# A graph attention layer: chunks attended to three slots later, turned tokens alternating with v, and another order on VectorE

## The chip, the cores and the metric

The kernel runs on one NeuronCore of one Trainium2 chip. The metric is the device time of one execution in microseconds (us). A core has TensorE (PE in the rows; PEld is its weight loads), VectorE (DVE), ScalarE (ACT), GpSimd (POOL) and SyncE (SP), which here only issues DMAs (SPq). Each engine works through its own instructions in the order written and waits on semaphores.

## What is computed

128 graphs of 128 nodes with 384 features go through a layer norm with relu, and one attention layer with 12 heads of 32 features, masked by the adjacency; the input is added at the end. Cut to what matters:

```python
h = relu(layernorm(x))                        # 128 graphs x 128 nodes x 384
q, k, v = (split_heads(h @ W + b) for W, b in ((Wq, bq), (Wk, bk), (Wv, bv)))
scores = einsum('bhqd,bhkd->bhqk', q, k) / sqrt(32) + beta * adj
scores = where(adj > 0, scores, -9e15)
out = x + merge_heads(softmax(scores) @ v)
```

## The kernel before, in words

**Words used.** A *group* is four graphs, 512 tokens; there are 32. A *chunk* is one graph and four of its heads, so a group has 12 chunks. A *step* s projects group s and attends to group s - 1; there are 33, of which the first only projects and the last only attends. Most steps are the body of a loop over pairs of steps (`run_steps`). A step has 12 *slots*, and in each slot TensorE does four things in this order: the scores of chunk n (L436, four matmuls), the turning (transposition) of the exponentials of chunk n - 1 (`turn_probs`, L444, four), a piece of the projections (`PIECES[u]`, L424), and the values of chunk n - 2 (`values_of`, L459 to L461, twelve short matmuls).

**Projections.** `UNITS` lists 13 units of a step: q and k, three each, nine matmuls of 512 columns per unit; v, four, nine matmuls of 384 columns; and three "turn" units, the transposed tokens of the next group (L404), four transposes each. The units are cut into twelve pieces of about equal cost. A unit is gathered in one of three banks (`ps_p`), so that `bank_free` lets unit o begin only when the unit three before it has been read out: for q and k that is VectorE's low part, for v ScalarE's copy, for a turn VectorE's low part of the tokens.

**Two parts.** q, k, the tokens and the probabilities are each kept as a high part, written by ScalarE, and a low part, the rest, written by VectorE (`low_part` L604, `turn_low` L594, `p_low` L630). v is copied by ScalarE (L525) and split by GpSimd (`split_v`, L318 and L320).

**A chunk's way.** TensorE's scores; VectorE adds the mask and takes the row maxima, head by head (`bias_scores`, L624); ScalarE takes the exponentials (`exps`, L510); TensorE turns them into `ps_t`, of which there is one bank; ScalarE takes the high part (`p_high`, L535) and VectorE the low one (`p_low`). `turn_probs` of a chunk waits for the exponentials of that chunk and for the `p_low` of the chunk before:

```python
pe.wait_ge(exp_done, HPC * (n + 1))
wait(pe, p_low_done, n)
```

After a graph's third chunk VectorE inverts the sums (L640) and scales (L645), GpSimd adds x (`add_x`, L326) and SyncE stores (L248).

**The spread.** The scores need q and k stacked by head. SyncE copies them there from SBUF to SBUF (`spread`, L241), 12 DMAs for q and 12 for k in a step, each set once the low parts of all three units are done. The scores of the first chunk of a group wait for both:

```python
if u == 0:
    pe.wait_ge(q_in, 16 * 3 * HPC * s)
    pe.wait_ge(k_in, 16 * 3 * HPC * s)
```

In the order before, that is slot 0 of the step after the one that projected the group. `q_st` and `k_st` have two buffers, by the parity of the step. On SyncE's queue a step is: the last store of two groups back, the load of x, the spread of q, a store, the load of the adjacency, the spread of k, two stores.

**VectorE in a slot.** Before: `bias_scores`, the inversion if a graph has ended, `p_low`, the scaling, one half of the mask (slots 4 and 7), `moments` (L571) of the next group's tokens, the low part of the unit that ended in the slot before, `variance` (L577).

Of the kernel before, what the change touches and what calls it, by code (L numbers as in the profile page):

```python
# [21 lines left out]
def graph_attention_kernel(nc, x, adj, wq, bq, wk, bk, wv, bv, beta, out):  # L22
# [3 lines left out]
    HPC = P // HD  # L26
# [4 lines left out]
    SLOTS = G * CH  # L31
    SCALE = float(HD) ** -0.5
# [8 lines left out]
             + [("v", 0), ("v", 1), ("turn", 0), ("v", 2), ("turn", 1), ("turn", 2), ("v", 3)])  # L41
# [37 lines left out]
    with ExitStack() as ctx:  # L79
# [132 lines left out]

        def rows_of(row):

            return row.rearrange("(o d) -> o d", o=1).broadcast_to([P, D])
# [6 lines left out]
        def _(sp):  # L222
# [27 lines left out]
            def step(s, par, looped=False):  # L250
                proj, attend = has(s, looped, 0, STEPS - 1), has(s, looped, 1, STEPS)
                if has(s, looped, 2, STEPS):
                    store(s - 2, G - 1)
# [15 lines left out]
                if attend:  # L269
                    store(s - 1, 1)  # L270
                    store(s - 1, 2)
                if s is STEPS:
                    store(s - 1, 3)
# [6 lines left out]
        def _(pool):  # L280
# [47 lines left out]
            def step(s, par, looped=False):  # L328
                proj, attend = has(s, looped, 0, STEPS - 1), has(s, looped, 1, STEPS)
                if proj:  # L330
                    add_bias(s, par, 0)
                    add_bias(s, par, 1)
                if has(s, looped, 2, STEPS):
                    add_x(s - 2, par, G - 1)
                if proj:
                    add_bias(s, par, 2)
                    add_bias(s, par, 3)
                if has(s, looped, 0, STEPS - 2):
                    rstd_of(s + 1)
                    normalise(s + 1, 1 - par)  # L340
                if attend:
                    add_x(s - 1, 1 - par, 0)
                if proj:
                    split_v(s, par, 0)
                if attend:
                    add_x(s - 1, 1 - par, 1)
                if proj:
                    split_v(s, par, 1)
                    split_v(s, par, 2)
                if attend:  # L350
                    add_x(s - 1, 1 - par, 2)
                if proj:
                    split_v(s, par, 3)
                if s is STEPS:
# [22 lines left out]
        def _(pe):  # L377
# [50 lines left out]
            def scores(s, par, u):  # L428

                j, c, n = u // CH, u % CH, SLOTS * (s - 1) + u  # L430
                if u == 0:
                    pe.wait_ge(q_in, 16 * 3 * HPC * s)
                    pe.wait_ge(k_in, 16 * 3 * HPC * s)
                wait(pe, biased_done, HPC * (n - 1))
                for i in range(HPC):
                    mm = pe.matmul(ps_s[u % 2][:, i * N:(i + 1) * N], q_st[0:STACK, 1 - par, i, c, j * N:(j + 1) * N],  # L436
                                   k_st[0:STACK, 1 - par, i, c, j * N:(j + 1) * N], start=True, stop=True)
# [9 lines left out]
            def values_of(g, vp, v, n, odd):  # L447
# [6 lines left out]
                for i in range(HPC):  # L454
# [3 lines left out]
                    first, second = v1[:, vp, j, h, :], v2[:, vp, j, h, :]  # L458
# [5 lines left out]
            def step(s, par, looped=False):  # L464
                proj, attend = has(s, looped, 0, STEPS - 1), has(s, looped, 1, STEPS)
                ahead = has(s, looped, 0, STEPS - 2)
                drain = 2 if not looped and s == STEPS else 0
                for u in range(SLOTS + drain):
                    n = SLOTS * (s - 1) + u
                    if attend and u < SLOTS:  # L470
                        scores(s, par, u)
                    if attend and u - 1 < SLOTS and (looped or n >= 1):
                        turn_probs(n - 1, (u - 1) % 2)
# [7 lines left out]
                    if attend and (looped or n >= 2):  # L481
                        late = u < 2
                        values_of(s - 1 - late, par if late else 1 - par, (u - 2) % SLOTS, n - 2, u % 2)
# [17 lines left out]
        def _(act):  # L501
            act.dma_start(xs[:, 0], x_v[0]).then_inc(x_in[0], 16)

            def exps(s, u):

                n, odd = SLOTS * (s - 1) + u, u % 2
# [252 lines left out]
```

## Time and profile before

| | us |
|---|---|
| median of 3 runs (lowest, highest) | 1191.81 (1189.29, 1191.97) |
| the profiled execution, its time | 1193.08 |
| its span in the trace | 1191.3 |
| TensorE busy in the span | 1068.0 (90%) |
| VectorE busy | 957.0 (80%) |
| ScalarE busy | 894.7 (75%) |
| GpSimd busy | 570.9 (48%) |
| mean granted TensorE clock | 0.969 |

The span is from the first to the last record of the trace; the run's own time is 1.8 us more. "Busy" counts the time between an instruction's start and end, so a matmul that overlaps the next counts with its drain; the start-to-start distance of matmuls (their pitch) tells what TensorE can do. A clock of 1.00 is 2.4 GHz, and half of that 1.2 GHz.

### The profile page before, as it was taken

How to read it: one execution, taken by the hardware profiler on the slowest of the kernel's cores; microseconds unless marked ns; L12 is line 12 of the kernel's file. 1: busy time of each engine (PE TensorE's matmuls, PEld its weight loads, DVE VectorE, ACT ScalarE, POOL GpSimd, SP SyncE). 2: the span in 40 equal slices, each digit the busy share in tenths (PEclk: the TensorE clock that was granted, in tenths of full speed). 3: DMA queues.
4: the chain of work that ended last, by engine and by line, in shares of the span. 5: the costliest groups of instructions: out<-in, count | busy, mean ns of one | idle time of the engine just before them, and what ended most of it. 6: DMA issues, size and time to landing. Idle time of an engine off the chain costs nothing.

```text
span 1191.3 us, 38643 instructions
## 1 busy us (share of the span) xinstructions
PE 1068.0 (90%) x10959; PEld 904.1 (76%) x10959; DVE 957.0 (80%) x4343; ACT 894.7 (75%) x2343; POOL 570.9 (48%) x756
## 2 busy tenths in 40 slices
PE   2799889999999999999999999999999999999875
PEld 1677777877787887778788777778877787888764
DVE  5478778888888888888888888878888888888764
ACT  2377768877787887777788787778877777887764
POOL 3735535445544545454454455454545445454421
PEclk9899999999999999999999999999999999999985
DMA  4434345444444544434554444454444345443330
GB/s 141 112 94 114 110 110 141 122 116 118 115 107 134 142 123 116 119 109 109 136 141 118 114 113 115 115 137 129 118 118 115 105 127 143 129 117 93 80 96 28
DMA packets 91030, 138.14 MB, mean 116 GB/s; under 512 B 15600, under 2 KB 66288, under 8 KB 90864
## 3 DMA queue, kind: packets, MB, share of 16 engines
q1 hardware_dynamic: 90336, 135.85, 42.4%
q14 instruction: 149, 1.22, 0.3%
q10 hardware_dynamic: 528, 0.79, 0.2%
q8 instruction: 17, 0.28, 0.1%
HBM read 35.91 MB, written 25.17 MB: 51 GB/s over the span
## 4 chain that ended last, share of the span: by engine, by line
PE 57%; SPq 14%; DVE 12%; issue 11%; DMA 5%; ACT 1%; POOL 1%; DVEq 1%; POOLq 0%; ACTq 0%
PE ps_p L424 35%; SPq L241 13%; PE ps_t L444 9%; PE ps_s L436 6%; DMA k_st<-kT 4%; DVE biased L624 4%; DVE kT L604 3%; PE ps_o L459 2%; PE ps_o L460 2%; PE ps_o L461 2%; DVE on L645 1%; DVE hT L594 1%; DMA beta_col<-in_L_gnn_beta 1%; PE ps_p L404 1%; ACT probs L510 1%
## 5 line engine op out<-in xcount | busy, mean ns | idle before, releaser
L624 DVE CUSTOM_DVE_ANT_0 biased<-ps_s,mask 128x128 f32<-128x128 f32 x1536 | 351.7, 284 | 181.0 <-PE ps_s L436 166.0
L510 ACT ACTIVATE probs<-biased,neg_max 128x128 f32<-128x128 f32 x1536 | 487.0, 391 | 7.4 <-DVE neg_max L624 7.0
L424 PE MATMUL ps_p<-hT,w 128*128 128x512 f32 x1728 | 475.2, 415 | 3.7 <-DVE w L733 3.7
L535 ACT ACTIVATE pT<-ps_t 128x512 f16<-128x512 f32 x384 | 229.3, 597 | 244.0 <-PE ps_t L444 242.9
L424 PEld LDWEIGHTS ps_p<-hT,w 128*128 128x128 f32 x1728 | 314.1, 193 | 61.5 <-issue 3.9
L630 DVE TENSOR_TENSOR pT<-ps_t,pT 128x512 f16<-128x512 f32 x384 | 256.9, 669 | 17.7 <-ACT pT L535 17.5
L444 PE MATMUL ps_t<-ident,probs 128*128 128x128 f32 x1536 | 241.6, 281 | 16.0 <-ACT probs L510 15.7
L326 POOL TENSOR_TENSOR on<-on,xb 128x384 f32<-128x384 f32 x128 | 128.5, 1004 | 264.4 <-DVE on L645 262.1
L424 PE MATMUL ps_p<-w,hT 128*128 128x384 f32 x1152 | 243.9, 348 | 0.0
L436 PE MATMUL ps_s<-k_st,q_st 96*128 96x128 f16 x1536 | 150.9, 221 | 55.6 <-DMA k_st<-kT 49.4
L424 PEld LDWEIGHTS ps_p<-w,hT 128*128 128x128 f32 x1152 | 193.5, 189 | 2.7
L318 POOL CAST v<-v_f 128x384 f16<-128x384 f32 x128 | 64.7, 505 | 267.4 <-ACT v_f L525 250.0
L459 PEld LDWEIGHTS ps_o<-v,pT 128*128 128x128 f16 x1536 | 123.8, 97 | 81.5 <-issue 53.9
L444 PEld LDWEIGHTS ps_t<-ident,probs 128*128 128x128 f32 x1536 | 166.2, 144 | 21.0 <-ACT probs L510 20.8
L459 PE MATMUL ps_o<-v,pT 128*128 128x33 f16 x1536 | 160.9, 181 | 1.1 <-DVE pT L630 1.1
L460 PE MATMUL ps_o<-v,pT 128*128 128x33 f16 x1536 | 155.7, 178 | 0.0
L461 PE MATMUL ps_o<-v,pT 128*128 128x32 f16 x1536 | 155.7, 177 | 0.0
L436 PEld LDWEIGHTS ps_s<-k_st,q_st 96*128 96x128 f16 x1536 | 90.6, 97 | 59.7 <-issue 59.7
L460 PEld LDWEIGHTS ps_o<-v,pT 128*128 128x128 f16 x1536 | 126.1, 97 | 1.1
L311 POOL TENSOR_TENSOR xb<-xs,bv_row 128x384 f32<-128x384 f32 x128 | 126.5, 1011 | 0.0
L624 DVE DVE_READ_ACCUMULATOR2_ANT neg_max<- 128x1 f32 x1536 | 126.5, 82 | 0.0
L461 PEld LDWEIGHTS ps_o<-v,pT 128*128 128x128 f16 x1536 | 124.2, 96 | 0.0
(59 smaller groups left out, 1073.0 us busy)
## 6 DMA issues: line engine op xcount, KB each, us to landing
q_st<-qT SPq DMA_DIRECT2D x384, 96.0 KB, 2.2
k_st<-kT SPq DMA_DIRECT2D x384, 96.0 KB, 2.1
out<-on SPq DMA_DIRECT2D x128, 192.0 KB, 1.9
xs<-in_x SPq DMA_DIRECT2D x31, 768.0 KB, 4.6
adjs<-in_adj SPq DMA_DIRECT2D x32, 256.0 KB, 2.9
xs<-in_x ACTq DMA_DIRECT2D x1, 768.0 KB, 6.9
k_st<-in_L_gnn_Wq SPq DMA_DIRECT2D x1, 576.0 KB, 5.3
k_st<-in_L_gnn_Wk SPq DMA_DIRECT2D x1, 576.0 KB, 7.4
```

The lines of the kernel that those rows point to most:

```text
L241: sp.dma_start(dst[HD * b:HD * (b + 1), par, i], src[HD * i:HD * (i + 1), part]).then_inc(landed, 16)
L326: pool.tensor_tensor(on[:, j % 2, :], on[:, j % 2, :], xb[:, par, j, :], ALU.add).then_inc(added, 1)
L424: mm = pe.matmul(dst, stationary, moving, start=m == 0, stop=m == MMS - 1)
L436: mm = pe.matmul(ps_s[u % 2][:, i * N:(i + 1) * N], q_st[0:STACK, 1 - par, i, c, j * N:(j + 1) * N], k_st[0:STACK, 1 - par, i, c, j * N:(j ...
L444: mm = pe.transpose(ps_t[:, i * N:(i + 1) * N], probs[:, odd, i, :], ident[:])
L459: pe.matmul(o, high, first, start=True, stop=False)
L460: pe.matmul(o, low, first, start=False, stop=False)
L461: mm = pe.matmul(o[:, 0:HD], high, second, start=False, stop=True)
L510: act.activation(probs[:, odd, i, :], biased[:, odd, i, :], ACT.Exp, bias=neg_max[:, odd, i:i + 1], scale=-1.0).then_inc(exp_done, 1)
L535: act.activation(pT[:, odd, 0], ps_t[:].rearrange("p (h q) -> p h q", q=N), ACT.Copy).then_inc(p_high_done, 1)
L624: dve.tensor_tensor_reduce(out=biased[:, odd, i, :], in0=ps_s[odd][:, i * N:(i + 1) * N], in1=mask[:, 1 - par, u // CH, :], scale=-1.0, sc ...
L630: dve.tensor_tensor(pT[:, odd, 1], ps_t[:].rearrange("p (h q) -> p h q", q=N), pT[:, odd, 0], ALU.subtract).then_inc(p_low_done, 1)
```

## The change

Scores of a chunk now come three slots later (`LAG = CH`): a group's chunks are scored in slots 3 to 11 of the step after its projection and in slots 0 to 2 of the one after that, and turning, values and scaling follow as before, one, two and three slots behind. The units `turn` and v alternate. On VectorE the low parts of projected units stand between `bias_scores` and `p_low`. The stores on SyncE and the additions and v splits on GpSimd are put where their data now come. The number of operations is the same. The core of the diff (`values_of`, `exps`, and `bias_scores` take their chunk from `chunk` likewise):

```diff
+    LAG = CH
...
     UNITS = ([("q", c) for c in range(CH)] + [("k", c) for c in range(CH)]
-             + [("v", 0), ("v", 1), ("turn", 0), ("v", 2), ("turn", 1), ("turn", 2), ("v", 3)])
+             + [("v", 0), ("turn", 0), ("v", 1), ("turn", 1), ("v", 2), ("turn", 2), ("v", 3)])
...
+        def chunk(s, par, u, behind, looped):
+
+            v = u - LAG - behind
+            back = 2 if v < 0 else 1
+            n = SLOTS * (s - 1) + v
+            if v >= SLOTS or (not looped and not 0 <= n < CHUNKS):
+                return None
+            return n, s - back, par if back == 2 else 1 - par, v % SLOTS
...
                 if has(s, looped, 2, STEPS):
-                    store(s - 2, G - 1)
+                    store(s - 2, 1)
+                    store(s - 2, 2)
+                if proj:
+                    spread(s, par, "q")
+                if has(s, looped, 2, STEPS):
+                    store(s - 2, 3)
                 if has(s, looped, 0, STEPS - 3):
...
-                if proj:
-                    spread(s, par, "q")
-                if attend:
-                    store(s - 1, 0)
                 if has(s, looped, 0, STEPS - 2):
                     sp.wait_ge(mask_done, s + 1)
                     sp.nop(nofuse=True)
                     sp.dma_start(adjs[:], adj_v[s + 1]).then_inc(adj_in, 16)
+                if attend:
+                    store(s - 1, 0)
                 if proj:
                     spread(s, par, "k")
...
+                for u in range(SLOTS + (LAG + 2 if s is STEPS else 0)):
+                    scored, turning, valued = (chunk(s, par, u, behind, looped) for behind in range(3))
+                    if scored:
+                        scores(*scored, (u - LAG) % 2)
+                    if turning:
+                        turn_probs(turning[0], (u - LAG - 1) % 2)
...
+                    scored, turning, _, valued = (chunk(s, par, u, behind, looped) for behind in range(4))
+                    ended = valued is not None and valued[3] % CH == CH - 1
+                    if scored:
+                        bias_scores(*scored, (u - LAG) % 2)
+                    if proj and u >= 1:
+                        low_parts(s, par, u - 1, ahead)
                     if ended:
-                        invert_sums(s - 1 - late, j)
-                    if attend and (looped or n >= 1) and u - 1 < SLOTS:
-                        p_low(n - 1, (u - 1) % 2)
+                        invert_sums(valued[1], valued[3] // CH)
+                    if turning:
+                        p_low(turning[0], (u - LAG - 1) % 2)
                     if ended:
-                        scale_out(s - 1 - late, j)
+                        scale_out(valued[1], valued[3] // CH)
...
                     if ahead and u < G:
                         moments(s + 1, 1 - par, u)
-                    if proj and u >= 1:
-                        low_parts(s, par, u - 1, ahead)
                     if ahead and u < G:
                         variance(s + 1, u)
```

In the rows of the order below (those that only handle registers are left out), `L624 ISA biased` is the masked score of one head and `L624 ISA neg_max` the read of its maximum; the lines of the changed kernel are some ten higher (L633 for L624, L639 for L630, L614 for L604, L604 for L594, L440 for L424, L452 for L436, L460 for L444, L420 for L404). VectorE in slot 2 of a step, from the last head's masked scores on, before:

```order
L624 ISA biased,neg_max<-ps_s,mask 128x128
L624 ISA neg_max 128x1
L640 RECIPROCAL inv_sum<-ps_o 128x12 [waits scaled,pv_done]
L630 TENSOR_TENSOR pT<-ps_t,pT 128x512 [waits p_high_done]
L645 TENSOR_TENSOR on<-ps_o,inv_sum 128x384 [waits stored1,inverted]
L571 BN_STATS stats<-xs 128x6 [waits var_done,x_in0]
L604 SCALAR_TENSOR_TENSOR qT<-ps_p,bias_qk,qT 128x512 [waits qk_high]
L575 REGISTER_ALU [waits rstd_done]
L577 BN_AGGR mean_var<-stats 128x2 [waits stats_done]
L196 REGISTER_ALU [waits scores_done]
L624 ISA biased,neg_max<-ps_s,mask 128x128 [waits exp_done]
```

and now:

```order
L633 ISA biased,neg_max<-ps_s,mask 128x128
L633 ISA neg_max 128x1
L614 SCALAR_TENSOR_TENSOR qT<-ps_p,bias_qk,qT 128x512 [waits qk_high]
L649 RECIPROCAL inv_sum<-ps_o 128x12 [waits scaled,pv_done]
L639 TENSOR_TENSOR pT<-ps_t,pT 128x512 [waits p_high_done]
L199 ISA [waits inverted]
L654 TENSOR_TENSOR on<-ps_o,inv_sum 128x384 [waits stored0]
L581 BN_STATS stats<-xs 128x6 [waits var_done,x_in0]
L585 REGISTER_ALU [waits rstd_done]
L587 BN_AGGR mean_var<-stats 128x2 [waits stats_done]
L199 REGISTER_ALU [waits scores_done]
L633 ISA biased,neg_max<-ps_s,mask 128x128 [waits exp_done,mask_done]
```

The low part of q (`qT`) stood after the scaling and the moments, between BN_STATS and BN_AGGR; it now stands ahead of `pT`, which is `p_low`, and BN_AGGR directly follows BN_STATS.

TensorE in slot 10 before, between the turned probabilities and the values:

```order
L444 MATMUL ps_t<-ident,probs 128x128 [waits p_low_done,exp_done]
L444 MATMUL ps_t<-ident,probs 128x128 x3
L424 MATMUL ps_p<-w,hT 128x384 x5
L404 MATMUL ps_p<-ident,hn 128x128 [waits normed,v_copied]
L404 MATMUL ps_p<-ident,hn 128x128 x3
L404 MATMUL ps_p<-ident,hn 128x128 [waits normed,h_low]
L404 MATMUL ps_p<-ident,hn 128x128 x3
L459 MATMUL ps_o<-v,pT 128x33 [waits p_low_done]
```

and now slots 8 and 10 in the same stretch:

```order
L460 MATMUL ps_t<-ident,probs 128x128 [waits p_low_done,exp_done]
L460 MATMUL ps_t<-ident,probs 128x128 x3
L440 MATMUL ps_p<-w,hT 128x384 x4
L418 ISA [waits qk_low]
L420 MATMUL ps_p<-ident,hn 128x128 [waits normed]
L420 MATMUL ps_p<-ident,hn 128x128 x3
L440 MATMUL ps_p<-w,hT 128x384 [waits qk_low]
L440 MATMUL ps_p<-w,hT 128x384 x2
```

```order
L460 MATMUL ps_t<-ident,probs 128x128 [waits p_low_done,exp_done]
L460 MATMUL ps_t<-ident,probs 128x128 x3
L440 MATMUL ps_p<-w,hT 128x384 x8
L420 MATMUL ps_p<-ident,hn 128x128 [waits normed,v_copied]
L420 MATMUL ps_p<-ident,hn 128x128 x3
```

The two turns that stood next to each other are apart, and v1 begins in slot 8 behind the first turn, where it waits for the bank of k's third unit (`qk_low`).

SyncE's queue in the loop, from the spread of q to the spread of k, before:

```order
L241 DMA q_st<-qT 32x1536 x11
L248 ISA [waits added]
L248 DMA out<-on 128x384
L266 ISA [waits mask_done]
L266 DMA adjs<-in_adj 128x4x128
L196 REGISTER_ALU [waits scores_done]
L241 DMA k_st<-kT 32x1536 [waits qk_low]
```

and now:

```order
L253 DMA q_st<-qT 32x1536 x11
L260 ISA [waits added]
L260 DMA out<-on 128x384
L275 ISA [waits xb_done,normed]
L275 DMA xs<-in_x 128x4x384
L279 ISA [waits mask_done]
L279 DMA adjs<-in_adj 128x4x128
L260 ISA [waits added]
L260 DMA out<-on 128x384
L199 REGISTER_ALU [waits scores_done]
L253 DMA k_st<-kT 32x1536 [waits qk_low]
```

The load of x and of the adjacency and the store of the group's first graph stand between the two spreads.

## Rows read from the trace of the kernel before

**Rows 1.** The page: the span.

```profile
span 1191.3 us, 38643 instructions
```

**Rows 2.** Busy time by stretch: us, PE, PEld, DVE, ACT, POOL, PEclk, DMA share, GB/s.

```profile
413.90:448.60 34.70, 32.36 (x342) 27.54 (x342) 29.40 (x135) 27.64 (x73) 17.75 (x24) 1.00 0.46 122
518.00:552.70 34.70, 33.75 (x342) 28.59 (x342) 27.97 (x134) 27.29 (x73) 16.01 (x21) 0.95 0.43 114
```

**Rows 3.** Waits of the whole span: us in total, times, longest us.

```profile
PEld ps_s L436 <- issue: 59.7, 34, 6.1
PE ps_s L436 <- DMA k_st<-kT: 49.4, 29, 5.8
```

**Rows 4.** Timeline of PE, slot 10 to slot 2: start, us, instructions, idle before.

```profile
409.19 0.66 PE L404 MATMUL ps_p<-ident,hn 128*128 128x128 f32 x4 [0.70 <-DVE hT L594]
...
409.99 0.38 PE L436 MATMUL ps_s<-k_st,q_st 96*128 96x128 f16 x4
...
413.99 0.39 PE L436 MATMUL ps_s<-k_st,q_st 96*128 96x128 f16 x4 [1.30 <-DMA k_st<-kT]
...
416.62 0.38 PE L436 MATMUL ps_s<-k_st,q_st 96*128 96x128 f16 x4
...
416.84 0.61 PE L444 MATMUL ps_t<-ident,probs 128*128 128x128 f32 x4
...
419.24 0.38 PE L436 MATMUL ps_s<-k_st,q_st 96*128 96x128 f16 x4
```

**Rows 5.** The chain of waits around 414 to 440: start, us until the next piece.

```profile
414.84 1.63 PE ps_p L424 x7
...
436.17 1.74 PE ps_p L424 x10
...
439.42 0.44 PE ps_p L404 x4
```

**Rows 6.** Timeline of SP's queue: the spreads of k, first and last of 30.

```profile
87.10 7.51 SPq L241 DMA_DIRECT2D k_st<-kT  x12
...
404.64 7.51 SPq L241 DMA_DIRECT2D k_st<-kT  x12
...
1102.32 8.39 SPq L241 DMA_DIRECT2D k_st<-kT  x12
```

**Rows 7.** The page: DMA issues, the spread of k, median us to landing.

```profile
k_st<-kT SPq DMA_DIRECT2D x384, 96.0 KB, 2.1
```

**Rows 8.** Timeline of DVE, slots 0 and 2.

```profile
416.19 0.55 DVE L571 BATCH_NORM_STATS2 stats<-xs 128x6 f32<-128x384 f32 x1
416.85 0.18 DVE L577 BATCH_NORM_AGGREGATE mean_var<-stats 128x2 f32<-128x6 f32 x1
...
419.86 0.29 DVE L624 CUSTOM_DVE_ANT_0 biased<-ps_s,mask 128x128 f32<-128x128 f32 x1 [0.31 <-PE ps_s L436]
...
420.86 0.63 DVE L630 TENSOR_TENSOR pT<-ps_t,pT 128x512 f16<-128x512 f32 x1
421.40 0.55 DVE L645 TENSOR_TENSOR on<-ps_o,inv_sum 128x384 f32<-128x384 f32 x1
421.86 0.55 DVE L571 BATCH_NORM_STATS2 stats<-xs 128x6 f32<-128x384 f32 x1
422.33 0.73 DVE L604 SCALAR_TENSOR_TENSOR qT<-ps_p,bias_qk,qT 128x512 f16<-128x512 f32 x1
422.98 0.17 DVE L577 BATCH_NORM_AGGREGATE mean_var<-stats 128x2 f32<-128x6 f32 x1
423.07 0.26 DVE L624 CUSTOM_DVE_ANT_0 biased<-ps_s,mask 128x128 f32<-128x128 f32 x1
```

**Rows 9.** Timeline of ACT in slot 1.

```profile
417.49 0.60 ACT L535 ACTIVATE pT<-ps_t 128x512 f16<-128x512 f32 x1 [0.77 <-PE ps_t L444]
```

**Rows 10.** Timeline of PE at the first and the last attention of a step.

```profile
60.95 0.58 PE L436 MATMUL ps_s<-k_st,q_st 96*128 96x128 f16 x4 [5.82 <-DMA k_st<-kT]
...
1148.63 0.38 PE L436 MATMUL ps_s<-k_st,q_st 96*128 96x128 f16 x4 [2.39 <-issue]
```

**Rows 11.** Timeline of ACT in the last step.

```profile
1152.46 0.60 ACT L535 ACTIVATE pT<-ps_t 128x512 f16<-128x512 f32 x1 [1.21 <-PE ps_t L444]
1152.96 1.26 ACT L510 ACTIVATE probs<-biased,neg_max 128x128 f32<-128x128 f32 x4
1155.43 0.60 ACT L535 ACTIVATE pT<-ps_t 128x512 f16<-128x512 f32 x1 [1.21 <-PE ps_t L444]
```

More of the change, by code:

```diff
@@ L329, in step @@
                 proj, attend = has(s, looped, 0, STEPS - 1), has(s, looped, 1, STEPS)
+                older = has(s, looped, 2, STEPS)
+                if has(s, looped, 1, STEPS):
+                    split_v(s - 1, 1 - par, G - 1)
                 if proj:
@@ L344, in step @@
                     split_v(s, par, 0)
+                    split_v(s, par, 1)
                 if attend:
@@ L426, in project, with scores @@
                     mm.then_inc(proj_done, 1)
[L428 to L433, printed above, removed]
+            def scores(n, g, gp, v, odd):
+                j, c = v // CH, v % CH
+                if v == 0:
+                    pe.wait_ge(q_in, 16 * 3 * HPC * (g + 1))
+                    pe.wait_ge(k_in, 16 * 3 * HPC * (g + 1))
                 wait(pe, biased_done, HPC * (n - 1))
                 for i in range(HPC):
-                    mm = pe.matmul(ps_s[u % 2][:, i * N:(i + 1) * N], q_st[0:STACK, 1 - par, i, c, j * N:(j + 1) * N],
-                                   k_st[0:STACK, 1 - par, i, c, j * N:(j + 1) * N], start=True, stop=True)
+                    mm = pe.matmul(ps_s[odd][:, i * N:(i + 1) * N], q_st[0:STACK, gp, i, c, j * N:(j + 1) * N],
+                                   k_st[0:STACK, gp, i, c, j * N:(j + 1) * N], start=True, stop=True)
                 mm.then_inc(scores_done, 1)
@@ L457, in values_of @@
                     high, low = pT[:, odd, 0, i, :], pT[:, odd, 1, i, :]
-                    first, second = v1[:, vp, j, h, :], v2[:, vp, j, h, :]
+                    first, second = v1[:, gp, j, h, :], v2[:, gp, j, h, :]
                     pe.matmul(o, high, first, start=True, stop=False)
@@ L464, in step @@
             def step(s, par, looped=False):
[L465 to L473, printed above, removed]
+                proj, ahead = has(s, looped, 0, STEPS - 1), has(s, looped, 0, STEPS - 2)
+                for u in range(SLOTS + (LAG + 2 if s is STEPS else 0)):
[4 more added lines that the diff above has]
+                        turn_probs(turning[0], (u - LAG - 1) % 2)
                     if proj:
@@ L480, in step @@
                                 turn(s + 1, ps_p[BANK[par][o]], UNITS[o][1])
-                    if attend and (looped or n >= 2):
-                        late = u < 2
-                        values_of(s - 1 - late, par if late else 1 - par, (u - 2) % SLOTS, n - 2, u % 2)
+                    if valued:
+                        values_of(*valued, (u - LAG) % 2)
             pe.wait_ge(consts_set, 3)
@@ L538, in step @@
             def step(s, par, looped=False):
-                proj, attend = has(s, looped, 0, STEPS - 1), has(s, looped, 1, STEPS)
-                ahead = has(s, looped, 0, STEPS - 2)
-                drain = 1 if not looped and s == STEPS else 0
-                for u in range(SLOTS + drain):
-                    n = SLOTS * (s - 1) + u
-                    if attend and (looped or n >= 1):
-                        p_high(n - 1, (u - 1) % 2)
-                    if attend and u < SLOTS:
-                        exps(s, u)
+                proj, ahead = has(s, looped, 0, STEPS - 1), has(s, looped, 0, STEPS - 2)
+                for u in range(SLOTS + (LAG + 1 if s is STEPS else 0)):
+                    scored, turning = (chunk(s, par, u, behind, looped) for behind in range(2))
+                    if turning:
+                        p_high(turning[0], (u - LAG - 1) % 2)
+                    if scored:
+                        exps(scored[0], (u - LAG) % 2)
                     if proj:
```

48 lines of the change are left out of this document (20 added, 28 removed).

## The prediction, made before the changed kernel ran

> **What bounds the kernel now.** I read the page, then the busy time by stretch, the waits, and the timeline of one step engine by engine. The span is 1191.3 us [rows 1]. In a step in the middle TensorE is busy for 32.36 of 34.70 us, VectorE for 29.40 and ScalarE for 27.64, at clock 1.00 [rows 2]: TensorE is nearest to the end and VectorE is not far. What TensorE waits for shows in the waits: the scores that open a step wait for the spread of k (49.4 us over 29 times, and under "issue" 59.7 us over 34 times for the same matmuls' weight loads; these overlap) [rows 3].
>
> What can a step cost at least? From the pitch of TensorE's instructions: seven matmuls of 512 columns go by in 1.63 us, 0.233 each; ten of 384 in 1.74, 0.174 each; four transposes in 0.44 [rows 5]. Scores take 0.22 us up to the turning [rows 4]. A slot with seven 512s is 2.62 us long (416.62 to 419.24) [rows 4], so scores, turning and values together are 2.62 - 1.63 = 0.99. A step is 54 x 0.233 + 36 x 0.174 + 3 x 0.44 + 12 x 0.99 = **32.0 us** of TensorE's work. From the spread of k in step 1 to that in step 30, 29 steps, it took 1102.32 - 87.10 = 1015.2 us [rows 6], **35.0 us** each. So 3.0 us of a step are waits. Two are seen: about 0.7 at the third turn, which waits for the first turn's low part to free its bank, and 1.3 (in other steps more) at the first scores of the next step, slot 11 having begun at 409.99 and lasting 2.56 by the pitch, with the next at 413.99, 1.4 late [rows 4]. Some steps run a stretch at half clock as well: mean clock 0.95 in one, against 1.00 [rows 2]. That clock loss follows waits and should go with them.
>
> **The change part by part.** *Three slots later.* The spread of k leaves SyncE from 404.64 for 7.51 us; its twelfth DMA is issued some 0.6 before that ends, at 411.5, and lands 2.1 later, at 413.6, and the scores begin at 413.99 [rows 4, 6, 7]. Now the scores need it three slots, 8 us, later. But the spread is itself set later: behind the store of the first graph, whose scaling is in VectorE's slot 8, with an addition on GpSimd of 1 us. I put its start at about 27 us into the step, its landing at 27 + 7.5 - 0.6 + 2.1 = 36, and its use at 34 + 8 = 42. Some 5 to 6 us are left, so this wait goes: -1.4 us or more a step.
>
> *Turns apart.* The second turn needs the bank of v0, long copied; the third that of v1. The 0.7 goes. Yet in slot 8 v1 now needs k's third unit, whose low part VectorE takes only in slot 8. Scores begin; 0.62 later VectorE can begin (419.24 to 419.86) [rows 4, 8]; masked scores 0.85, low part 0.65 [rows 8]; so the bank is free at 2.2, while TensorE is there after 0.22 + 0.36 + 4 x 0.174 + 0.44 = 1.7. A wait of 0.5, and as VectorE comes 0.25 late into slot 8 (below) and TensorE restarts slowly, **0.9**. In slot 9 v2 needs the first turn's low part in the same way: **0.2**.
>
> *Low parts first.* In slot 2 VectorE's masked scores and inversion take 1.00 us (419.86 to 420.86), `p_low` and scaling 1.00, moments 0.47, low part 0.65, variance 0.09 [rows 8]: 3.21, the next masked scores starting at 423.07. Now BN_AGGR follows BN_STATS at once, and such a pair takes 0.66 (416.19 to 416.85) plus 0.09 [rows 8] instead of 0.56: 0.2 more in slots 2 and 3. So slot 2 is 3.4 and slot 3 2.9, against TensorE's 2.85 and 2.62: VectorE enters slot 3 0.55 and slot 4 0.8 late. Before, that delay hit low parts, which nobody waited for soon. Now `p_low` ends in slot 3 at 0.62 + 0.55 + 0.85 + 0.65 + 0.69 = 3.4 after the scores, and TensorE wants to turn the next chunk at 2.62 + 0.22 = 2.84: a wait of **0.6** in slot 4. In slot 5 the same sum leaves **0.3**, and in slots 8 and 0, which follow slots with the mask or with an ended graph, **0.2** each. Where VectorE is on time, the sum is 0.62 + 0.85 + 0.65 + 0.69 = 2.81, just in time: this edit has no margin.
>
> *ScalarE.* It takes the turned chunk 0.65 after the turning starts (416.84 to 417.49) [rows 4, 9], then the exponentials; 0.65 + 0.5 + 1.3 = 2.45 is below a slot, so it hides behind TensorE. GpSimd is busy for 17.75 of 34.70 [rows 2]; its additions and splits in the new places have several us before their use. The load of x is behind the spread of q and a store, and still some 12 us early. All three cost nothing; should GpSimd be late, the store and then the spread of k are late next, with the 5 us above.
>
> **The step.** 32.0 + 0.6 + 0.3 + 0.9 + 0.2 + 0.2 = 34.2 (the wait in slot 0 of 0.2 is partly the same delay; I count it once with slot 8's), so **34.2** against 35.0.
>
> **The ends.** At the first attention TensorE has idled for 5.82 us [rows 10]; three slots of projections, 22 x 0.233 = 5.1 us, now fit there. Counted from 60.95, step 1 ends three slots, 8.1 us, sooner. The last step has 15 chunks instead of 12 to pass through the chain ScalarE and TensorE alone, 2.97 us each (1152.46 to 1155.43) [rows 11]: 8.9 more. Step 31 has no turns, -1.5 as before.
>
> **Sum.** Before, 60.95 to 1148.63 [rows 10] is 31 steps at 35.1. Now 60.95 + 31 x 34.2 - 8.1 - 1.5 + (1191.3 - 1148.63) + 8.9 = 1163. The profiled run's time was 1.8 above its span and 1.3 above the median of the runs, so the median should be **1164**, 28 us or 2.3% less.
>
> **Bounds.** The unknown is what TensorE waits in a step under the new order. If VectorE's delay is half of what I work out, the step is 33.1 and the time 1164 - 31 x 1.1 = 1130. If each of the waits is a quarter longer and the restarts cost more, it is 34.85: 1184.
>
> **Rivals.** *TensorE runs free.* If VectorE catches up (its 29.4 us of work fit into 32), the step is about 32.4 and the time 1164 - 31 x 1.8 = 1108. Against it: VectorE's work is not even, and slots 2 to 5 hold 11.4 us of it against 10.7 of TensorE's. 0.13.
>
> *A page's rule.* The row of the mid step gives the weight loads 27.54 us against the matmuls' 32.36 [rows 2]. The Trainium skill (Perfetto Trace Analysis, Identifying the Most-Contended Engine) holds matmul busy time to be a poor measure of TensorE's distance from its limit and weight-load busy time to be a good one. By it TensorE has 7 us to give, VectorE's 29.4 would bound the step, and the time would be 1164 - 31 x 4.8 = 1015. The pitch speaks against that here: 0.233 us a matmul with nothing waited for [rows 5]. 0.01.
>
> *Slower: the turning always waits for `p_low`.* The low part ahead of it stands in nine slots. Each costs at most its own 0.65: 5.9 us, a step of 37.9 and 1164 + 31 x 3.7 = 1279. It turns slower once these nine waits exceed 0.35 us each (35.1 - 32.0 = 3.1). The place is L444 waiting for L630. For it: the sum above is 2.81 against 2.84. Against it: only slots 2 to 5 are fuller than TensorE's. 0.07.
>
> *The wait stays.* If the spread of k starts over 5 us later than I put it (its store or the addition ahead is late), the change does not do what it says: a step stays at 35.0, about 1190, the last step's 8.9 made up by the first's 8.1. 0.05.
>
> **The numbers.** My forecast has 0.74. A difference of 0.3% (3.6 us) is about what runs of this kernel can tell. Faster: 0.71 of the forecast's 0.74, with 0.14 of the first two rivals, is 0.85, and mild forms of the two slow rivals make it 0.87. Same: 0.05. Slower: 0.08. 1130 to 1184 leaves out the free case, the slow one and the tails.
>
> **What would show it.** Right: no wait of the first scores for DMA k_st in the loop; spreads of k 34.2 us apart; TensorE waiting for DVE pT (`p_low`) at the turning in slots 4 and 5, and for DVE kT at v1; the clock 1.00 in every step; the last step 8.9 us longer. Wrong: waits for k_st remain; steps of 32.4, with hardly a wait of TensorE; or waits of the turning in all slots.

## The result and the profile after

| | before | changed kernel |
|---|---|---|
| median, us (lowest, highest) | 1191.89 (1189.29, 1193.88) | 1257.4 (1255.43, 1263.74) |
| ratio, 95% interval | 1 | 1.0562 (1.0529 to 1.0595) |
| span in the trace | 1191.3 | 1254.4 |
| TensorE, VectorE, ScalarE busy | 90%, 80%, 75% | 88%, 78%, 71% |
| mean granted TensorE clock | 0.969 | 0.961 |

The change made the kernel 5.6% slower; 1164 was forecast, with 1130 to 1184 as the range. The page of the changed kernel:

```profile
span 1254.4 us, 38643 instructions
...
PE 1103.8 (88%) x10959; PEld 920.9 (73%) x10959; DVE 972.7 (78%) x4343; ACT 896.2 (71%) x2343; POOL 581.5 (46%) x756
...
q14 instruction: 97, 0.79, 0.2%
```

Every engine has as many instructions as before, and all are idle for longer. TensorE's busy time is 36 us more than the 1068.0 before, for the same matmuls. Its waits (us in total, times, longest):

```profile
PEld ps_t L460 <- ACT probs L522: 102.6, 58, 4.5
PE ps_t L460 <- ACT probs L522: 71.3, 28, 4.3
DVE biased L633 <- issue: 69.2, 41, 5.2
ACT probs L522 <- DVE neg_max L633: 66.8, 41, 4.5
PE ps_t L460 <- DVE pT L639: 34.4, 72, 0.8
PE ps_p L440 <- DVE kT L614: 9.8, 31, 0.7
```

The wait of the scores for k's spread (49.4 us [rows 3]) is gone, as forecast, and the small waits for `p_low` and for k's low part are there. But one chain has grown: TensorE's turning waits 71.3 us for ScalarE's exponentials (15.7 before), these wait for VectorE's row maxima, and VectorE waits for nothing the profile knows ("issue"). SyncE's queue shows where it falls (start, duration of the spreads of k):

```profile
376.11 7.52 SPq L253 DMA_DIRECT2D k_st<-kT  x12
417.54 7.50 SPq L253 DMA_DIRECT2D k_st<-kT  x12
452.11 7.53 SPq L253 DMA_DIRECT2D k_st<-kT  x12
493.52 7.50 SPq L253 DMA_DIRECT2D k_st<-kT  x12
```

The steps are no longer alike: 34.6 us and 40.6 to 41.4 us in turn. The busy time of one of each (columns as in [rows 2]):

```profile
417.54:452.11 34.57, 33.15 (x344) 27.79 (x343) 29.83 (x136) 27.66 (x75) 17.80 (x24) 1.00 0.46 122
452.11:493.52 41.41, 35.61 (x344) 29.58 (x343) 29.87 (x136) 27.78 (x75) 17.77 (x24) 0.92 0.38 102
```

The same instructions, 6.8 us more, and part of the long step at half clock. Inside it, on VectorE, on ScalarE and on TensorE, one timeline fence each:

```profile
458.47 0.54 DVE L654 TENSOR_TENSOR on<-ps_o,inv_sum 128x384 f32<-128x384 f32 x1
464.03 0.29 DVE L633 CUSTOM_DVE_ANT_0 biased<-ps_s,mask 128x128 f32<-128x128 f32 x1 [5.02 <-issue]
```

```profile
464.37 1.28 ACT L522 ACTIVATE probs<-biased,neg_max 128x128 f32<-128x128 f32 x4 [4.31 <-DVE neg_max L633]
```

```profile
458.51 0.38 PE L452 MATMUL ps_s<-k_st,q_st 96*128 96x128 f16 x4
...
461.13 0.38 PE L452 MATMUL ps_s<-k_st,q_st 96*128 96x128 f16 x4
465.71 1.10 PE L460 MATMUL ps_t<-ident,probs 128*128 128x128 f32 x4 [4.20 <-ACT probs L522]
466.46 3.33 PE L440 MATMUL ps_p<-hT,w 128*128 128x512 f32 x7
```

VectorE runs nothing for 5.02 us (459.01 to 464.03). The scores it needs are those of slot 0, started at 458.51; 0.62 later, at 459.13, it could have begun. TensorE goes on to the next scores (461.13), then stands for 4.2 us, because it wants to turn the chunk of slot 0. After that seven matmuls take 3.33 us where this row reads 1.88 before (at 449.34): the granted clock from 466.46 to 469.7 is 0.50. The place is always the same: between the last instruction of a pair of steps and the first of the next, VectorE's branch back to the start of the loop. The queue of instruction packets carries two within VectorE's gap (window 459.2 to 464.03):

```profile
q14 instruction: 2, 0.02, 0.9%
```

Before, that branch was there too, and VectorE stood for 1.89 us after the low parts. But the scores that it needed next were late as well, by their wait for k. VectorE and TensorE of the kernel before, at its back edge:

```profile
446.98 1.28 DVE L594 SCALAR_TENSOR_TENSOR hT<-ps_p,hT 128x512 fp32r<-128x512 f32 x2
450.15 0.29 DVE L624 CUSTOM_DVE_ANT_0 biased<-ps_s,mask 128x128 f32<-128x128 f32 x1 [1.89 <-issue]
```

```profile
448.74 0.39 PE L436 MATMUL ps_s<-k_st,q_st 96*128 96x128 f16 x4 [1.68 <-DMA k_st<-kT]
```

The scores came so late that VectorE could not have begun before 448.74 + 0.62 = 449.36 in any case: the branch delayed it by 0.8 us, where it is 4.9 us in the changed kernel. What that made of a step shows in the spreads of k, two of which enclose this edge (439.13 and 474.04):

```profile
439.13 7.51 SPq L241 DMA_DIRECT2D k_st<-kT  x12
474.04 7.51 SPq L241 DMA_DIRECT2D k_st<-kT  x12
508.54 7.50 SPq L241 DMA_DIRECT2D k_st<-kT  x12
```

With the one at 404.64 [rows 6] these are 34.5, 34.9 and 34.5 us apart. The step with the edge is 0.4 us longer, and three times in the whole run it is 36.2.

The theory to test: every back edge of VectorE makes it fetch its instructions anew, 2 to 5 us; before, most of that lay under the wait for k, which the change took away.

### The profile page after: what moved, and what is told of

Same layout as the page of the kernel before. It is cut to its first block and busy times, and to the rows that moved or that the text cites. A ratio compares the mean times of both kernels' runs of the same rounds, so it can differ in the third digit from the quotient of the medians.

```text
span 1254.4 us, 38643 instructions
## 1 busy us (share of the span) xinstructions
PE 1103.8 (88%) x10959; PEld 920.9 (73%) x10959; DVE 972.7 (78%) x4343; ACT 896.2 (71%) x2343; POOL 581.5 (46%) x756
## 5 line engine op out<-in xcount | busy, mean ns | idle before, releaser
L633 DVE CUSTOM_DVE_ANT_0 biased<-ps_s,mask 128x128 f32<-128x128 f32 x1536 | 354.1, 286 | 215.5 <-PE ps_s L452 140.2
L440 PE MATMUL ps_p<-hT,w 128*128 128x512 f32 x1728 | 480.7, 419 | 3.2 <-DVE w L740 3.2
L440 PEld LDWEIGHTS ps_p<-hT,w 128*128 128x128 f32 x1728 | 319.5, 197 | 62.6 <-issue 3.5
L460 PE MATMUL ps_t<-ident,probs 128*128 128x128 f32 x1536 | 248.9, 287 | 108.1 <-ACT probs L522 71.3
L639 DVE TENSOR_TENSOR pT<-ps_t,pT 128x512 f16<-128x512 f32 x384 | 255.8, 666 | 23.6 <-ACT pT L547 22.4
L460 PEld LDWEIGHTS ps_t<-ident,probs 128*128 128x128 f32 x1536 | 169.3, 146 | 131.5 <-ACT probs L522 102.6
L440 PE MATMUL ps_p<-w,hT 128*128 128x384 f32 x1152 | 253.3, 351 | 9.8 <-DVE kT L614 9.8
L440 PEld LDWEIGHTS ps_p<-w,hT 128*128 128x128 f32 x1152 | 194.0, 189 | 24.1 <-DVE kT L614 17.2
L452 PE MATMUL ps_s<-k_st,q_st 96*128 96x128 f16 x1536 | 150.6, 221 | 2.6 <-DMA k_st<-kT 2.6
L633 DVE DVE_READ_ACCUMULATOR2_ANT neg_max<- 128x1 f32 x1536 | 126.8, 83 | 0.0
L333 POOL TENSOR_TENSOR v<-v_f,v 128x384 f16<-128x384 f32 x128 | 114.0, 890 | 10.3
L318 POOL TENSOR_SCALAR hn<-xs,neg_mean,rstd 128x384 f32<-128x384 f32 x128 | 92.8, 737 | 8.0 <-POOL rstd L310 8.0
```

The costliest lines, as they stand in the source:

```text
L440: mm = pe.matmul(dst, stationary, moving, start=m == 0, stop=m == MMS - 1)
L452: mm = pe.matmul(ps_s[odd][:, i * N:(i + 1) * N], q_st[0:STACK, gp, i, c, j * N:(j + 1) * N], k_st[0:STACK, gp, i, c, j * N:(j + 1) * N], ...
L460: mm = pe.transpose(ps_t[:, i * N:(i + 1) * N], probs[:, odd, i, :], ident[:])
L633: dve.tensor_tensor_reduce(out=biased[:, odd, i, :], in0=ps_s[odd][:, i * N:(i + 1) * N], in1=mask[:, gp, v // CH, :], scale=-1.0, scalar= ...
L639: dve.tensor_tensor(pT[:, odd, 1], ps_t[:].rearrange("p (h q) -> p h q", q=N), pT[:, odd, 0], ALU.subtract).then_inc(p_low_done, 1)
```

## Experiments: is it the back edge?

**Both kernels with all 33 steps written out.** In `run_steps`, for every engine:

```diff
-            step(0, 0)
-            step(1, 1)
-            with eng.Fori(1, STEPS // 2 - 1) as pair:
-                step(2 * pair, 0, True)
-                step(2 * pair + 1, 1, True)
-            step(STEPS - 2, 0)
-            step(STEPS - 1, 1)
-            step(STEPS, 0)
+            for s in range(STEPS + 1):
+                step(s, s % 2)
```

> The changed kernel with its 33 steps written out, so that no engine branches back; nothing else differs. Theory A (VectorE stands still for 5.0 us at the loop's back edge, every second step, while its instructions are fetched again, and nothing covers that now): the 5 us stall and the half clock after it vanish, spreads of k are 34.6 us apart throughout, time 1257 - 14 x 6.3 = about 1169. Theory B (the long step has its cause in the traffic or in the order of waits, not in the loop): time stays at 1257.

Measured: 1164.46 us (1163.52 to 1165.22), ratio to before 0.9779 (0.9759 to 0.9799), with the changed kernel's work and no branch. The loop alone is 93 us of the changed kernel's 1257.4.

> The kernel before with its steps written out. Theory A: there the scores' wait for the spread of k covered nearly all of the fetch at the back edge, so at most 14 x 1.3 us are won: 1173 to 1192. Theory B: 1192, unchanged.

Measured: 1201.08 us, ratio 1.009 (1.0069 to 1.011): the kernel before gains nothing from being written out, it loses 0.9%, which neither theory had. Its spreads of k:

```profile
370.91 7.51 SPq L235 DMA_DIRECT2D k_st<-kT  x12
405.08 7.89 SPq L235 DMA_DIRECT2D k_st<-kT  x12
439.69 8.86 SPq L235 DMA_DIRECT2D k_st<-kT  x12
476.80 8.96 SPq L235 DMA_DIRECT2D k_st<-kT  x12
514.04 7.50 SPq L235 DMA_DIRECT2D k_st<-kT  x12
```

Where SyncE gets the twelve DMAs out in 7.5 us, the next spread follows after 34.2 us; where it takes 8.9, after 37.1 or 37.2. In the looped kernel 28 of 31 spreads take 7.5. In the old order the scores wait for k, so such a delay lands on the path. So this run does not tell what the edge cost before; the 0.4 us above do. Why SyncE is slower when written out is open.

**Only one side written out.** VectorE alone (its `run_steps(dve, step)` replaced by the plain loop above), and all the others with VectorE looped:

> The changed kernel with VectorE's 33 steps written out and the other engines' loops as they are. Theory (VectorE's back edge alone makes the long steps): no long steps, spreads of k 34.1 to 34.4 us apart throughout, 1164 us (1160 to 1172), as with all engines written out. Rival 1 (the back edge of TensorE or of ScalarE, which fetch their instructions anew as well): every second step stays near 41 us, 1230 to 1257. Rival 2 (each engine's edge adds a part): 1185 to 1230.

Measured: 1163.83 us (1163.24 to 1164.4), ratio 0.9784 (0.9761 to 0.9807).

> The changed kernel with TensorE, ScalarE, GpSimd and SyncE written out, and only VectorE in a loop of two steps. Theory (VectorE's back edge alone): steps of 34.6 and 41 us in turn, 5.0 us without an instruction on VectorE at every second step, 1250 to 1262 us. Rival (TensorE's or ScalarE's edge): 1164 to 1180.

Measured: 1257.6 us, spreads of k at 416.78, 451.37, 492.86 and 527.44. So it is VectorE's back edge, wholly; those of TensorE, ScalarE, GpSimd and SyncE cost nothing here. The page of the kernel with VectorE alone written out:

```profile
q14 instruction: 51, 0.42, 0.1%
```

The packets fall from 97 to 51 though a straight run has the same instructions to fetch: the loop had fetched 46 more. Its 14 iterations have 13 back edges (the trace has 13 such gaps, of 4.7 to 5.2 us), so that is 3.5 packets an edge. VectorE stands for two of them; the others come while it works.

**Half as many back edges.** Four steps to an iteration instead of two, on every engine:

```diff
-            with eng.Fori(1, STEPS // 2 - 1) as pair:
-                step(2 * pair, 0, True)
-                step(2 * pair + 1, 1, True)
+            with eng.Fori(0, (STEPS - 4) // 4) as quad:
+                for k in range(4):
+                    step(4 * quad + 2 + k, k % 2, True)
```

> The changed kernel with four steps to an iteration in place of two, on every engine: 7 back edges instead of 14. Theory (a cost for each back edge, 6.6 us by the difference between 41.0 and 34.4): 1257 - 7 x 6.6 = 1211 us, and 1190 where the new position of the loop in memory makes the stall 2.9 us as in the kernel shifted by 64 instructions. Rival (steps with waits against registers are slow in themselves, wherever the edge): 1250 to 1260.

Measured: 1211.79 us, with one step in four long and six gaps instead of 13. Waits against registers in the looped steps cost nothing that shows.

**The kernel before without its cover.** VectorE's branch moved in the kernel before, from the start of slot 0 to between slots 2 and 3 (its loop then runs from slot 3 of a step to slot 2 of the step two later):

```diff
-            run_steps(dve, step)
+            step(0, 0)
+            step(1, 1)
+            step(2, 0, False, 0, 3)
+            with dve.Fori(1, STEPS // 2 - 1) as pair:
+                step(2 * pair, 0, True, 3, SLOTS)
+                step(2 * pair + 1, 1, True)
+                step(2 * pair + 2, 0, True, 0, 3)
+            step(STEPS - 2, 0, False, 3, SLOTS)
+            step(STEPS - 1, 1)
+            step(STEPS, 0)
```

> The kernel before, with VectorE's back edge moved from the start of slot 0, where TensorE waits for the spread of k anyway, to between slots 2 and 3 of a step. Theory (the edge was paid before as well, and hidden by the wait for k's spread): the stall of VectorE shows as 2 to 5 us at slot 3, where nothing hides it, and 14 of them make 1191 + 14 x 3 = 1233 us (1215 to 1255). Rival (the edge cost nothing in the old order because of what VectorE runs there, or the changed order itself makes it cost): 1188 to 1196 us.

Measured: 1223.82 us against 1188.49 of the kernel before on that chip. The same work in the same order, 35 us more, because the branch now stands where nobody waits anyway. VectorE at one of the 13 edges, which last 2.6 to 2.8 us:

```profile
471.51 0.29 DVE L624 CUSTOM_DVE_ANT_0 biased<-ps_s,mask 128x128 f32<-128x128 f32 x1 [2.60 <-PE ps_s L436]
```

This is the cover shown directly: the back edge had been there all along. But uncovered it costs the kernel before 35 us, and the changed kernel 93. The rest must come from something else than the lost cover.

**The same move in the changed kernel**, and its loop moved in memory by 64 small memsets ahead of it on VectorE (`dve.memset(scratch[:, i:i + 1], 0.0)`, written before its first wait):

> The changed kernel with VectorE's back edge between slots 2 and 3 instead of between slots 11 and 0; the order of its operations is the same, and at that point only one store is in flight. Theory A2: VectorE's stall falls to 2.5 us or less, time about 1210 to 1225. Theory A1 or a fixed fetch time: it stays between 3 and 5 us; time 1225 to 1265. Theory B: nothing changes at slots 11 to 0.

> The changed kernel with 64 tiny memsets on VectorE ahead of everything (they run while it waits for its first input), which moves its loop by 64 instructions, half of one fetched block. Theory A1 (how long the stall is hangs on where the branch and its target lie in the fetched blocks): VectorE's idle time at the back edge differs from 5.0 us by over 0.5 us, time 1200 to 1290. Theory A2 (the fetch stands behind the spread of k in the DMA queues): it stays at 5.0 us and the time at 1257, plus or minus 4.

Measured: 1240.07 and 1221.8 us. The stalls on VectorE, first with the branch at slot 3, then with the shift:

```profile
467.78 0.29 DVE L633 CUSTOM_DVE_ANT_0 biased<-ps_s,mask 128x128 f32<-128x128 f32 x1 [3.18 <-issue]
```

```profile
447.77 0.54 DVE L655 TENSOR_TENSOR on<-ps_o,inv_sum 128x384 f32<-128x384 f32 x1
451.19 0.29 DVE L634 CUSTOM_DVE_ANT_0 biased<-ps_s,mask 128x128 f32<-128x128 f32 x1 [2.88 <-PE ps_s L453]
```

64 instructions more, and 36 us less. A second theory had the fetch stand behind the spread of k in the DMA queues; it wanted 2.5 us or less with the branch at slot 3, and an unchanged 5.0 with the shift, and got neither. The last row names TensorE's scores as what VectorE waited for, but TensorE had started them at 447.56 and taken 0.38 for them; it is the same stall, under another name. In this gap (448.3 to 451.19) the instruction queue carries one packet instead of two:

```profile
q14 instruction: 1, 0.01, 0.7%
```

**A whole block, and a quarter.** A packet of this queue is 0.79 MB / 97, some 8 KB. If it matters where in such a block of 128 instructions the loop lies, 128 memsets (with which the page counts 98 packets instead of 97) must bring the long stall back:

> The changed kernel, looped, with 128 small memsets on VectorE at its start, so that its loop lies one block of 128 instructions (8192 bytes, the size of an instruction packet in the trace) later. Theory (the stall at the back edge depends on where in a block the loop begins and ends): as without the shift, a stall of 5.0 us and 1250 to 1265 us. Rival (any shift helps, the first one by accident of something else): the stall stays 2.9, 1215 to 1230.

> As before with 32 memsets, a quarter of a block. Theory (place in a block): a stall of 5.0 or of 2.9 us, or between, by which side of a block's border an instruction falls; 1215 to 1262 us, and not outside. Rival (place does not matter): the same stall as with 128.

Measured: 1260.7 us with 128 and 1208.68 with 32. On VectorE, at the back edge, of the kernels with 128 and with 32:

```profile
467.11 0.29 DVE L634 CUSTOM_DVE_ANT_0 biased<-ps_s,mask 128x128 f32<-128x128 f32 x1 [4.75 <-issue]
```

```profile
448.68 0.29 DVE L634 CUSTOM_DVE_ANT_0 biased<-ps_s,mask 128x128 f32<-128x128 f32 x1 [2.81 <-PE ps_s L453]
```

128 is as good as none. Together, in the table: the price of an edge is the time less 1164.5, divided by the number of edges (for the last row, the time less 1188.5). The last column is an estimate: the gap, plus what the clock costs. At half clock TensorE takes nearly twice as long (the seven matmuls above: 3.33 us for 1.88), so half of the time spent there is taken as lost; counted is what lies beyond that of the kernel written out, by edge. The time at half clock is 2 x (1 - mean clock) x span, 51 us for the kernel written out (mean clock 0.978).

| kernel | gap on VectorE, us | mean clock | time, us | edges | price of one, us | gap and clock, us |
|---|---|---|---|---|---|---|
| changed kernel | 5.02 | 0.961 | 1257.4 | 13 | 7.1 | 6.8 |
| 128 memsets ahead | 4.75 | 0.959 | 1260.7 | 13 | 7.4 | 6.8 |
| four steps to an iteration | 5.23 | 0.969 | 1211.8 | 6 | 7.9 | 7.2 |
| branch at slot 3 | 3.18 | 0.954 | 1240.1 | 13 | 5.8 | 5.6 |
| 64 memsets ahead | 2.88 | 0.968 | 1221.8 | 13 | 4.4 | 3.9 |
| 32 memsets ahead | 2.81 | 0.976 | 1208.7 | 13 | 3.4 | 3.1 |
| kernel before, branch at slot 3 | 2.60 | 0.972 | 1223.8 | 13 | 2.7 | 2.8 |

So an edge costs one or two waits of about 2.5 us for a packet, by where the loop lies, and on top what TensorE loses at half clock after its pause. The packets say the same: the three kernels with 32 or 64 memsets or the branch at slot 3 have 84 in the queue, 13 fewer than the changed kernel's 97, one for each edge. Their number is no price by itself, though: the kernel before has 149, and which engine fetches the rest is not told. Open is why the clock falls so differently behind nearly equal gaps (0.954 and 0.976), and at which position the gap changes: three shifts don't map it. All rows but the first are single runs.

## Experiments: what are the parts of the change worth?

All of these have the steps written out, so that no branch disturbs, and stand against 1164.46.

**The old order of units** (v, v, turn, v, turn, turn, v in `UNITS`):

> The changed kernel with all 33 steps written out (1164.46 us, steps of 34.1 to 34.4), and in it the old order of units: v, v, turn, v, turn, turn, v. Theory (the prediction's sum): v1 no longer stands behind k's third low part (its wait of some 0.9 us goes), the first turn does and comes one v later (0 to 0.2), and the third turn waits again for the first turn's low part, but that is now taken before p_low (0 to 0.3 instead of 0.7). The step becomes 33.4 to 33.9, the time 1140 to 1156. Rival (the turn's wait of 0.7 comes back whole and the wait for k's low part only moves): 1160 to 1172.

Measured: 1172.06 us (1171.43 to 1172.1), 7.6 more than with the new order, which is the rival. The 0.7 to 0.8 us for v1 go, but a turning waits in a new place:

```profile
432.46 0.63 PE L454 MATMUL ps_t<-ident,probs 128*128 128x128 f32 x4 [0.59 <-DVE pT L633]
```

It is in slot 0 (scores at 431.49). Two turns end together in slot 10, so VectorE has two low parts ahead of `p_low` in slot 11, and the turning of slot 0 waits for that one. The wait only moved.

**VectorE's old order** (inversion, `p_low`, scaling, moments, then the low parts):

> The changed kernel with all steps written out, and in it VectorE's old order: inversion, p_low, scaling, moments, then the low parts. Theory (the sum): the waits of the turning for p_low go (measured 0.75 and 0.29 us in slots 4 and 5 and 0.13 to 0.16 in two others, 1.3 in all), and v1 and v2 wait for low parts 0.6 us longer each, 1.2 in all: a step of 34.1 +- 0.3, 1152 to 1172 us. Rival (low parts first is what made the steps shorter): 1180 to 1195. Rival on the other side (the low parts are wanted late enough, the order only costs): 1125 to 1145.

Measured: 1193.47 us (1191.36 to 1195.18), 29 more, which is the first rival. The wait that grew (9.9 us before this edit):

```profile
PE ps_p L434 <- DVE kT L608: 53.0, 31, 2.1
```

and TensorE in slot 8 of one step, and in slot 9 of another:

```profile
465.03 0.80 PE L434 MATMUL ps_p<-w,hT 128*128 128x384 f32 x3 [1.70 <-DVE kT L608]
```

```profile
433.88 0.44 PE L434 MATMUL ps_p<-w,hT 128*128 128x384 f32 x1 [0.53 <-DVE hT L598]
```

The turning's waits did go, as reckoned. But in slot 8 a graph has ended, so not only `p_low` but also inversion and scaling stand ahead of k's last low part, some 1.2 us instead of 0.6: v1 waits 1.70 where it waited 0.31, and v2 0.53 where it had not waited. By the starts of the scores, on the mean over the steps, slot 8 lasts 4.61 us instead of 3.39 and slot 9 3.62 instead of 2.75: 2.1 more, against 1.2 saved in slots 4, 5 and 0. That is 0.9 a step, 28 of the 29 us. I had priced the one side by its rows and the other by a rule of thumb.

**One slot later instead of three** (`LAG = 1`):

> The changed kernel with all steps written out, and chunks attended to one slot later instead of three. Theory: the spread of k lands 5.3 us before its use (lands 431.8, used 437.1), and two slots are 5.4: it lands just when it is used, a wait of 0 to 0.5 us a step; the last step has two chunks less at 2.97 each, the first two slots of 2.7 less of cover. 1164 to 1182 us. Rival (three slots are needed, the wait for k comes back with restarts at half clock): 1182 to 1200.

Measured: 1160.94 us (1159.99 to 1161.78), below both ranges. Hardly a wait for k comes, and the steps are 34.04 us each (four steps from 392.77 to 528.94) against 34.15. One slot is enough to take the wait for k away. The 3.5 us (0.3%) that it gains over three slots were measured on two different chips; they are too few to build on.

**A version from both findings.** The trace says where low parts first pay (slots 8 to 11, for v1 and v2) and where they cost (slots 4 and 5, where VectorE is late for `p_low`). So they go first only there:

```diff
                     if scored:
                         bias_scores(*scored, (u - LAG) % 2)
-                    if proj and u >= 1:
+                    if proj and u >= 8:
                         low_parts(s, par, u - 1, ahead)
...
+                    if proj and 1 <= u < 8:
+                        low_parts(s, par, u - 1, ahead)
                     if ahead and u < G:
                         variance(s + 1, u)
```

> The changed kernel with all steps written out, and VectorE's low parts ahead of p_low in slots 8 to 11 only; in slots 0 to 7 they stand where they stood before. Theory (low parts first pay where v1 and v2 wait for their bank and cost where VectorE is late): the turning waits of slots 4 and 5 go (0.75 and 0.29 us, 1.04 a step), the waits for kT stay 0.3 to 0.9 as in the changed kernel: steps of 33.1 us, 1164.5 - 31 x 1.04 = 1132 us (1126 to 1142). Rival (VectorE's lateness in slots 2 to 5 comes from its load and not from the order; it only moves to slot 8, whose low part is then late): 1155 to 1175.

Measured: 1133.31 us (1132.19 to 1133.95), ratio to before 0.9514 (0.9482 to 0.9546). This version beats both kernels, and the sum of rows, 1132, held within 2 us. Its spreads of k:

```profile
413.42 9.33 SPq L247 DMA_DIRECT2D k_st<-kT  x12
446.51 8.14 SPq L247 DMA_DIRECT2D k_st<-kT  x12
```

Steps of 33.1 us. One more wait gone was hoped for with `LAG = 1` on top:

> The kernel of the run before this one, with chunks attended to one slot later instead of three. Theory: the same 3.5 us less as without the change of order (1160.94 against 1164.46): 1129 us (1122 to 1139). Rival (with shorter steps the spread of k lands too late for one slot, the wait for k comes back): 1140 to 1165.

Measured: 1141.61 us (1138.96 to 1142.43), 8 us slower: the rival. With shorter steps one slot no longer always covers the spread. Slot 0, at whose end the first scores of a group are due, lasts 2.9 us or more in 14 of 30 steps, against 2.7 in the others; together that is the 8 us. Most of these waits are of 0.2 to 1.0 us; the longest:

```profile
466.58 0.38 PE L446 MATMUL ps_s<-k_st,q_st 96*128 96x128 f16 x4 [1.83 <-issue]
```

The profile names no releaser here; that it is k is worked out. That spread left SyncE from 455.22 to 462.76, its last DMA some 0.6 before the end, so it would have landed at 464.3 with the 2.1 us of [rows 7]. The page of the stretch from 460 to 466.6 has this for its DMAs:

```profile
k_st<-kT SPq DMA_DIRECT2D x5, 96.0 KB, 3.8
```

3.8 us to land, among other transfers, makes 466.0, and the scores start at 466.58. So the two gains don't add up: one lives on the slack that the other uses.

## Why the prediction was wrong, point by point

**The step that failed** is the sum: "60.95 + 31 x 34.2". It took the steps to be alike and the two halves of the loop with them. From "29 steps, it took 1102.32 - 87.10 = 1015.2 us [rows 6], 35.0 us each", the waits of a step were put down to the third turn and to k's spread ("1.3 (in other steps more)"). In every second step VectorE's branch stood there as well: 1.89 us labelled "issue", of which the late scores hid all but 0.8; the step grew by 0.4. When the cover went, nothing was hidden any more, and the gap itself was two waits for a packet instead of one. Together the 13 edges cost 93 us, and the sum has no term for them. In the best place of the loop that was tried (32 memsets ahead) they still cost 44 us, and the kernel is then at 1208.7, slower than before as well; the other 49 us hang on where this build happened to put the loop.

The sum should have asked the question it asks of other things it costs at nothing: what hides this, and what does it cost without? The waits of the kernel before hold the hint, in a line that was not among the rows:

```profile
DVE biased L624 <- issue: 11.7, 6, 2.1
```

The 59.7 us under "issue" in [rows 3] are no such hint: they are TensorE's own weight loads, in the same wait for k.

The trace agrees with a page that the prediction did not use. The Trainium skill (Runtime: NRT & Kernel Launch, Instruction fetch mechanics) says that prefetch is sequential, and that a taken branch to a block that is no longer held has to wait for a fetch. It gives no price; the gaps in the table give 2.6 to 5.2 us. It speaks of blocks of 16 KiB; the packets of the queue on which VectorE's come are of 8 KB here.

**The terms that held**, by the kernel written out, where the branch is absent. TensorE in one of its steps:

```profile
440.10 0.38 PE L446 MATMUL ps_s<-k_st,q_st 96*128 96x128 f16 x4
441.07 0.63 PE L454 MATMUL ps_t<-ident,probs 128*128 128x128 f32 x4 [0.59 <-DVE pT L633]
...
443.49 0.38 PE L446 MATMUL ps_s<-k_st,q_st 96*128 96x128 f16 x4
...
446.41 0.38 PE L446 MATMUL ps_s<-k_st,q_st 96*128 96x128 f16 x4
...
451.82 0.38 PE L446 MATMUL ps_s<-k_st,q_st 96*128 96x128 f16 x4
...
454.24 0.80 PE L434 MATMUL ps_p<-w,hT 128*128 128x384 f32 x3 [0.31 <-DVE kT L608]
455.20 0.38 PE L446 MATMUL ps_s<-k_st,q_st 96*128 96x128 f16 x4
```

- Slot 4 is 3.39 us (440.10 to 443.49) instead of 2.62: a wait of 0.77, forecast 0.6. Slot 5 is 2.92: 0.30, forecast 0.3.
- Slot 8 is 3.38 for 7 x 0.174 + 0.44 + 0.99 = 2.65 of work: 0.73, forecast 0.9. The waits of 0.2 in slots 9 and 0 are there at 0.1 and 0.2.
- The wait for k is gone, and with `LAG = 1`, 5.2 us less of cover, hardly any came back: the 5 to 6 us of slack were there.
- The step is 34.15 on the mean, forecast 34.2; the whole 1164.46, forecast 1164.0.
- The last step, from its first scores (1111.60) to the end of the span, is 7.9 us longer than before, forecast 8.9.
- So each term of a step held within 0.2 us (slot 4 was longer and slot 8 shorter than forecast, and these cancel), and the forecast was 93 us off by one that was missing.

**The rivals.** The slower one (the turning waits for `p_low` in all nine slots, 1279 us) is nearest to the time, but for another reason: the turning waits 0.3 to 0.8 us in few slots, not in nine. The wait for k did not stay. TensorE does not run free, though the version with the mixed order comes half way (33.1 against 32.0 of work).

**What would have shown it** was partly right: no wait for k, the waits for `p_low` and for kT at v1. Spreads of k 34.2 us apart and a clock of 1.00 in every step failed, and failed in every second step, which points to the loop at once.

## What to carry to other kernels

When a change takes away a wait, list what else lies at the same moment on the other engines: a loop's back edge, a slow restart or a late queue may have been hidden by it, and becomes the bound. In a looped kernel read both halves of the body apart, and look for gaps labelled "issue" at the iteration's border before a cadence is taken for the sum. If an engine's loop body is fetched anew at each branch, write that engine out alone, or try the branch or the body at another place, before the schedule is judged.

## What the runs showed that was not expected

- VectorE's uncovered back edge costs 2.6 to 5.2 us of standing still, and 2.7 to 7.9 us of time, since TensorE restarts at its lower clock level (granted 0.50 from 466.46 to 469.7, 0.92 on the mean of the long step).
- Its size hangs on the loop's place in memory: 5.0 us with no shift, 2.9 with 64 instructions, 2.8 with 32, 4.8 with 128. Unrelated instructions ahead of a loop can move a kernel by 49 us (1257.4 to 1208.7).
- TensorE's, ScalarE's, GpSimd's and SyncE's back edges cost nothing measurable (1257.6 with them written out, 1257.4 with them looped; and 1163.83 with them looped, 1164.46 with them written out).
- Written out, SyncE needs up to 9.8 us for twelve DMA issues that mostly take 7.5 in the loop (7.5 also where VectorE alone is written out); it matters only where the spread is waited for.
